# First attention of a two-layer model: k's halves swapped per key tile, projections moved behind score products

## The reference

```python
h = _layernorm(x, axis=-1) * (1 + ca) + sa
x = x + ga * _L0_attn_ref(h, ...)
...
x = _rmsnorm(tokens, norm_w)
q = (x @ Wq).reshape(b, n, QH, DH).transpose(0, 2, 1, 3)
kv = x @ Wkv
k = kv[..., :H * DH].reshape(b, n, H, DH).transpose(0, 2, 1, 3)
v = kv[..., H * DH:].reshape(b, n, H, DH).transpose(0, 2, 1, 3)
q = _mh_rmsnorm(q, q_gamma)
k = _mh_rmsnorm(k, k_gamma)
q = q.reshape(b, H, g, n, DH)
sim = jnp.einsum('bhgid,bhjd->bhgij', q, k)
sim = jnp.tanh(sim / SOFTCLAMP) * SOFTCLAMP
sim = sim * DH ** (-0.5)
sim = jnp.where(causal, neg, sim)
attn = jax.nn.softmax(sim, axis=-1)
out = jnp.einsum('bhgij,bhjd->bhid', attn, v)
out = out.transpose(0, 2, 1, 3).reshape(b, n, H * DH)
return out @ Wout
```

## Time and profile before

| | us |
|---|---|
| median of 3 runs | 1952.88 (1952.42 to 1953.05) |
| profiled execution | 1955.93, of it span 1954.2 |
| PE busy | 1891.4 (97%) |
| PE weight loads | 1323.5 (68%) |
| VectorE busy | 1588.3 (81%) |
| ScalarE busy | 1443.6 (74%) |
| GpSimd busy | 674.2 (35%) |

### The profile page before, as it was taken

The page is one execution under the profiler, slowest core; times in us unless marked ns, Lnnn a source line. Parts: engine busy times, 40 slices in busy tenths (PEclk is TensorE's granted clock), DMA queues, the critical chain, the costliest instruction groups (busy, mean ns, idle before and its releaser), DMA issues. The chain is left out here.

```text
span 1954.2 us, 41236 instructions
## 1 busy us (share of the span) xinstructions
PE 1891.4 (97%) x14878; PEld 1323.5 (68%) x14878; DVE 1588.3 (81%) x3865; ACT 1443.6 (74%) x2020; POOL 674.2 (35%) x956
## 2 busy tenths in 40 slices
PE   7999999999999999998899999899999978999998
PEld 4788888888888888887344444677777753444443
DVE  6888888888888888873776775699999977888886
ACT  3888888888888888884677777466767755666665
POOL 1555555555555555552000000255555540000000
PEclk7999999999999999998999999899999999999999
DMA  2501111011110111100675554100000000000000
GB/s 96 127 22 28 29 28 28 15 28 29 29 28 15 29 28 29 26 23 1 138 174 119 111 120 99 45 2 2 2 3 2 2 2 6 12 11 17 12 17 17
DMA packets 57001, 75.67 MB, mean 39 GB/s; under 512 B 9456, under 2 KB 34144, under 8 KB 56672
## 3 DMA queue, kind: packets, MB, share of 16 engines
q1 hardware_dynamic: 56800, 73.03, 15.7%
HBM read 51.47 MB, written 4.77 MB: 29 GB/s over the span
## 5 line engine op out<-in xcount | busy, mean ns | idle before, releaser
L513 PE MATMUL a_pS<-qs,k 128*128 128x256 f16 x1536 | 377.2, 273 | 3.7 <-issue 2.6
L533 PEld LDWEIGHTS a_pO<-va,pr 128*128 128x128 f32 x2048 | 322.9, 192 | 82.1 <-issue 72.9
L533 PE MATMUL a_pO<-va,pr 128*128 128x66 f32 x2048 | 332.3, 252 | 3.1 <-DVE on L857 2.5
L1083 POOL TENSOR_SCALAR_AFFINE_SELECT pr<-pr 128x512 f32<-128x512 f32 x256 | 181.7, 734 | 192.4 <-ACT pr L1009 192.3
L1001 ACT ACTIVATE th<-a_pS 128x1536 f32<-128x1536 f32 x128 | 185.8, 1451 | 68.1 <-PE a_pS L513 65.2
L1982 ACT ACTIVATE c_pr<-c_pS 128x2048 f32<-128x2048 f32 x96 | 180.4, 1879 | 59.8 <-PE c_pS L1785 59.8
L2026 POOL TENSOR_SCALAR_AFFINE_SELECT c_pr<-c_pr 128x512 f32<-128x512 f32 x256 | 155.5, 638 | 181.9 <-DVE c_pr L1875 181.9
L513 PEld LDWEIGHTS a_pS<-qs,k 128*128 128x128 f16 x1536 | 196.3, 131 | 7.3 <-issue 4.0
L864 POOL TENSOR_TENSOR qp<-qg,qp 128x1024 f16<-128x1024 f32 x64 | 149.2, 2331 | 121.5 <-ACT qp L977 121.5
L1009 ACT ACTIVATE pr<-th 128x1536 f32<-128x1536 f32 x128 | 189.6, 1481 | 1.1
L535 PEld LDWEIGHTS a_pO<-va,pr 128*128 128x128 f32 x1024 | 162.5, 192 | 31.4 <-issue 28.7
(11 more groups left out here) (267 smaller groups left out, 4336.2 us busy)
## 6 DMA issues: line engine op xcount, KB each, us to landing
b_cwB<-b_by_expert SPq DMA_DIRECT2D x64, 512.0 KB, 8.5
k<-k SPq DMA_DIRECT2D x64, 256.0 KB, 3.7
x<-in_L_attn_tokens_dram SPq DMA_DIRECT2D x8, 512.0 KB, 6.9
out_dram<-x SPq DMA_DIRECT2D x16, 256.0 KB, 2.3
mb<-a_by_sample SPq DMA_DIRECT2D x31, 128.0 KB, 3.5
d_h<-in_L_ffn_h_w_dram SPq DMA_DIRECT2D x2, 1024.0 KB, 8.2
c_gb<-c_by_sample SPq DMA_DIRECT2D x1, 2048.0 KB, 8.3
b_by_expert<-b_cwT SPq DMA_DIRECT2D x64, 8.0 KB, 1.4
```

The costliest lines, as they stand in the source:

```text
L513: last = pe.matmul(out, (k1, k2)[part][k][:, h // G2, keys * P:(keys + 1) * P], q, start=part == 0, stop=part == 1)
L533: last = pe.matmul(out, w[:, hh * N + t * P:hh * N + (t + 1) * P], v[:, 0, p, :], start=True, stop=t == 0)
L1083: last = gp.affine_select(out=own, in_=own, compare_op=ALU.is_ge, fill=0.0, base=0, pattern=[[0, HPG], [1, P]], channel_multiplier=-1)
```

## The change

Four things in `attention0`:

1. `k1` and `k2` are laid out by key tile first, and SP swaps k's halves in two transfers per key tile, each pair issued as soon as that tile's copy is done. Score product 0 of a sample waits for the copy of tile 0 alone, product 1 for its transfers, product 4 for the copy of tile 1 and product 5 for its transfers.
2. The loop of PE is written out in another order; so are those of VectorE, ScalarE and GpSimd, which begin at another point of the sample. The calls are the same and as many.
3. The banks are given out in another way, and with them the waits at the head of the calls.
4. `act_take_k` writes its tile of `k1` as one run of 1024 elements.

```diff
-        k1 = [sb(f'k1{k}', [P, KH, N], F16) for k in range(2)]
+        k1 = [sb(f'k1{k}', [P, TT, KH, P], F16) for k in range(2)]
...
-        QK_BANK = (1, 0, 1, 1, 0, 2)
+        QK_BANK = (1, 0, 1, 2, 1, 2)
...
-                sp.wait_ge(s_ks, 2 * n + 2)
-                sp.dma_start(k2[k][0:DH, :, :], k1[k][DH:P, :, :]).then_inc(s_k2, 16)
-                sp.dma_start(k2[k][DH:P, :, :], k1[k][0:DH, :, :]).then_inc(s_k2, 16)
+                for t in range(TT):
+                    sp.wait_ge(s_ks, 2 * n + t + 1)
+                    sp.dma_start(k2[k][0:DH, t, :, :], k1[k][DH:P, t, :, :]).then_inc(s_k2[t], 16)
+                    sp.dma_start(k2[k][DH:P, t, :, :], k1[k][0:DH, t, :, :]).then_inc(s_k2[t], 16)
...
             elif m == 3:
                 if n >= 1:
+                    pe.wait_ge(s_ks, 2 * n)
+            elif m == 4:
+                if n >= 1:
                     pe.wait_ge(s_qs, 4 * n - 3)
...
-                    pe.wait_ge(s_k2, 32 * (n + 1))
+                    pe.wait_ge(s_ks, 2 * n + 1)
...
+            if g == 0:
+                if m == 1:
+                    pe.wait_ge(s_k2[0], 32 * (n + 1))
+                elif m == 4:
+                    pe.wait_ge(s_ks, 2 * n + 2)
+                elif m == 5:
+                    pe.wait_ge(s_k2[1], 32 * (n + 1))
...
-                pe_weigh(pe, n, 1, 10)
-                pe_project_qk(pe, n + 2, 3)
-                pe_weigh(pe, n, 1, 11)
                 pe_project_qk(pe, n + 2, 4)
                 pe_project_qk(pe, n + 2, 5)
...
-            act.activation(k1[n % 2][:, :, t * P:(t + 1) * P], pW[KT_BANK[t]][:, :].bitcast(F16).rearrange('p (h i) -> p h i', i=P), ACT.Copy).then_inc(s_ks, 1)
+            act.activation(k1[n % 2][:, t, :, :], pW[KT_BANK[t]][:, :].bitcast(F16).rearrange('p (h i) -> p h i', i=P), ACT.Copy).then_inc(s_ks, 1)
```

More of the change, by code:

```diff
@@ L355, in attention0 @@
         s_qt, s_qs, s_kt, s_ks = (sem(x) for x in ('qt', 'qs', 'kt', 'ks'))
[L356 removed]
+        s_v, s_va = (sem(x) for x in ('v', 'va'))
+        s_k2 = [sem(f'k2{t}') for t in range(TT)]
         s_sc, s_th, s_pr, s_mk, s_pv, s_rl, s_on, s_as = (
@@ L404, in pe_values @@
             if t == 0:
+                if n >= 1:
+                    pe.wait_ge(s_qs, 4 * n - 1)
+                else:
+                    pe.wait_ge(s_hT, n + 2)
+            else:
                 if n + 1 < B:
@@ L417, in pe_project_qk @@
             if m == 0:
-                pe.wait_ge(s_hT, n + 1)
+                if n >= 1:
+                    pe.wait_ge(s_qg, 6 * n - 1)
             elif m == 1:
-                if n >= 2:
-                    pe.wait_ge(s_qs, 4 * n - 5)
+                if n >= 1:
+                    pe.wait_ge(s_va, 2 * n - 1)
+                else:
+                    pe.wait_ge(s_hT, n + 1)
+            elif m == 2:
+                if n >= 3:
+                    pe.wait_ge(s_at, 2 * n - 4)
                 elif n >= 1:
-                    pe.wait_ge(s_qg, 6 * n - 1)
-            elif m == 2:
-                if n >= 1:
                     pe.wait_ge(s_va, 2 * n)
@@ L455, in pe_turn_k @@
                 if n + 1 < B:
[L456 to L459, removed]
-                if n + 1 < B:
                     pe.wait_ge(s_qg, 6 * n + 8)
                 else:
-                    pe.wait_ge(s_qs, 4 * n - 1)
+                    pe.wait_ge(s_va, 2 * n + 1)
+            else:
+                if n >= 2:
+                    pe.wait_ge(s_og, n - 1)
+                elif n >= 1:
+                    pe.wait_ge(s_qs, 4 * n)
+                else:
+                    pe.wait_ge(s_qg, 6 * n + 6)
             out = pW[KT_BANK[t]][:, :].bitcast(F16)
@@ L474, in pe_turn_q @@
             if i == 0:
-                pe.wait_ge(s_ks, 2 * n + 1)
+                if n + 1 < B:
+                    pe.wait_ge(s_qg, 6 * n + 9)
+                else:
+                    pe.wait_ge(s_at, 2 * n - 2)
             elif i == 1:
-                pe.wait_ge(s_ks, 2 * n + 2)
+                if n >= 2:
+                    pe.wait_ge(s_st, 3 * n - 5)
+                else:
+                    pe.wait_ge(s_ks, 2 * n + 1)
             elif i == 2:
-                if n + 1 < B:
-                    pe.wait_ge(s_qg, 6 * n + 11)
+                if n + 2 < B:
+                    pe.wait_ge(s_hT, n + 3)
                 else:
@@ L512, in pe_score @@
                 out, q = pS[:, hh * N:(hh + 1) * N], qs[k][:, h, :]
-            last = pe.matmul(out, (k1, k2)[part][k][:, h // G2, keys * P:(keys + 1) * P], q, start=part == 0, stop=part == 1)
+            last = pe.matmul(out, (k1, k2)[part][k][:, keys, h // G2, :], q, start=part == 0, stop=part == 1)
             if m == SCORES - 1:
@@ L547, in pe_heads_back @@
                     else:
-                        pe.wait_ge(s_st, 3 * n - 2)
+                        pe.wait_ge(s_og, n)
                 else:
-                    pe.wait_ge(s_at, 2 * n + 1)
+                    if n + 2 < B:
+                        pe.wait_ge(s_va, 2 * n + 6)
+                    elif n + 1 < B:
+                        pe.wait_ge(s_qs, 4 * n + 5)
+                    else:
+                        pe.wait_ge(s_at, 2 * n)
             last = pe.transpose(pW[HB_BANK[t]][:, j * P:(j + 1) * P], as_[:, t, j * P:(j + 1) * P], c.id32[:, :])
@@ L579, in pe_out_back @@
                 pe.wait_ge(s_og, n + 1)
-                pe.wait_ge(s_og, n + 1)
+                if n + 2 < B:
+                    pe.wait_ge(s_ks, 2 * n + 5)
+                elif n + 1 < B:
+                    pe.wait_ge(s_qs, 4 * n + 7)
+                else:
+                    pe.wait_ge(s_st, 3 * n - 2)
             last = pe.transpose(pW[BACK_BANK][:, t * P:(t + 1) * P], og[:, t * P:(t + 1) * P], c.id32[:, :])
@@ L657, in _ @@
                 pe_turn_k(pe, n + 1, 0)
-                pe_score(pe, n, 3, 2)
-                pe_weigh(pe, n, 1, 6)
-                pe_score(pe, n, 3, 3)
+                for m in range(1, 6):
+                    pe_score(pe, n, 3, m)
+                    pe_weigh(pe, n, 1, m + 1)
                 if n == -1:
@@ L711, in _ @@
                 pe_weigh(pe, n, 3, 0)
[L712 to L719 removed]
+                pe_turn_q(pe, n + 1, 2)
+                pe_turn_q(pe, n + 1, 3)
+                for m in range(0, 11):
+                    pe_score(pe, n + 1, 1, m)
+                    pe_weigh(pe, n, 3, m + 1)
+                pe_score(pe, n + 1, 1, 11)
+                pe_values(pe, n + 2, 0)
+                pe_heads_back(pe, n, 0, 0)
+                pe_values(pe, n + 2, 1)
+                pe_weigh(pe, n + 1, 0, 0)
+                pe_score(pe, n + 1, 2, 0)
+                pe_weigh(pe, n + 1, 0, 1)
+                pe_score(pe, n + 1, 2, 1)
+                pe_weigh(pe, n + 1, 0, 2)
         def dve_ln(dve, n, step):
```

216 lines of the change are left out of this document (86 added, 130 removed).

## The result

The changed kernel takes 1922.44 us in the median (four runs, 1920.92 to 1925.79), the one before 1952.65 beside it. The ratio is 0.9848, 95% interval 0.9831 to 0.9865: faster by 30.2 us, where 25.8 were forecast. Run again later on one chip with the kernel before, it took 0.9844 (0.9829 to 0.9860) of it. The profiled execution took 1925.79 us (span 1924.0), the slowest of its four.

A forecast was written before the change was run, and what follows sets the result against it. TensorE's instruction stream was taken as the bound, 26.95 us a sample. Order 23.5 plus swap 3.8 less new waits 1.5 gave 25.8 us: 1930.1 profiled, 1927 in the median, range 1921 to 1942.

The forecast's parts named there:

- The cost of an f32 instruction behind a short one: TensorE's stream: f32 straight behind a weighing product or turn pays 0.053 us; reordering saves 0.78 a sample, 23.5 us.
- P after S: A projection straight after a score product on TensorE: taken as 0.86 us, between bounds of 0.86 and 0.91.
- the rival in which the projection still pays: Projections behind scores on TensorE still pay 0.053 each; 11 us not won, 1938 us; chance 0.16.
- full cover by loads pulled ahead: TensorE's weight loads always hidden, so order is free; only the swap's 3.8 us remain, 1949 us; chance 0.04.
- The swap: A sample's first score product waits for transfers of k's halves; splitting them wins 3.8 us, at worst none.
- the spare time: Between k's transfers landing and the score needing them: 1.3 us spare in the median, 0.5 at the slowest landing.
- New waits, -1.5: TensorE waiting for ScalarE's tanh between score groups: 0.05 us once a sample, 1.5 us lost; bounds 0 and 13.
- The spare time claimed: Blocks between score groups: tanh needs 1.81 us, blocks last 2.00, 2.04 and 2.11, so 0.2 to 0.3 spare.
- Filling and draining counted at nothing: First and last samples of the stage: TensorE also waits for other engines there, so no gain was counted.
- short pairs: f32 instructions straight after a weighing product or turn on TensorE: 15 a steady sample before, none after.
- VectorE as the bound: Rival: VectorE, 23.1 us of work a sample, has its waits add up and becomes the limit; 1960 us, chance 0.05.

The follow-up runs named there:

- The three kernels that bring it back: Changed kernel with five weighing products behind weighing products: 1928.97 us; three output products behind weighing products: 1926.34 us; two projections behind weighing products: 1926.36 us.
- the kernel that had the drain's clock at 1.00: Kernel before, with ten idle transpositions filling TensorE's 1.16 us wait in the last sample: 1950.94 us, ratio 0.9996 to the kernel before.

## Why the prediction was right, and where it was off

**The cost of an f32 instruction behind a short one: right, in rule and in size.** The three kernels that bring it back give 0.053 (W), 0.052 (O) and 0.053 (P). "P after S" was a value chosen between bounds of 0.86 and 0.91; it is 0.86, so the rival in which the projection still pays falls, and with it full cover by loads pulled ahead. The Trainium skill, "TensorE: Matmul & The Clock Gate", Step-by-step: what each phase is for, states that the next tile's weights load while this tile's matmul runs. With weighing products in pairs PE's stream lengthens by 0.26 us a sample and PE waits for nothing, so as full cover that doesn't hold for these short matmuls; the measurement decides. The term was 0.78 a sample, and 26.84 less 26.07 is 0.77.

**The swap: right in the size, too simple in the reason.** 3.8 us of waits are gone, 3.5 of them seen alone in the 28 intervals, and 0.95 in the last sample that the forecast hadn't counted. But I priced it as an amount in the kernel before. In the new order the same whole transfers would cost 14.6 us, since the first score of a sample comes 0.3 sooner after k's second copy. The forecast missed nothing by this, because the changed kernel has the split; with the order alone I'd have been 10 us wrong, as the expectation for that kernel was. The half-size transfer, priced like the whole (3.7), lands in 2.3, so by the forecast's own sum the spare time was 2.7 and not 1.3.

**New waits, -1.5: mis-sized, none came.** From 88 to 850 us the view lists not one idle interval of PE. The spare time claimed, 0.2 to 0.3 at three places, is 0.12 at one and 0.23 at two; the value of 0.05 a sample was caution, not a reading.

**Filling and draining counted at nothing: the main miss.** The step was "PE also waits for other engines, so I count nothing there". The forecast took 15 short pairs in each of 30 samples, 450. The stage has 505 before and 28 after, 477 fewer; 461 to 465 fewer show their 0.05, since waits cover some. That is 0.6 to 0.8 us more than forecast. The last sample's wait for the swap went as well. Both could have been counted as in the body. At equal clock the tail brought 2.0 us, net of new waits for the tanh; another 3.3 come from the clock, which was lower before in that one profile.

**The sum.** For the profiled executions: 25.2 in the body against a predicted 0.91 by 28, 25.5; plus 6.5 at both ends, less 1.6 in later stages, 30.1. For the medians: 30.2 against 25.8. The forecast had 25.5 for the body and 0.3 for the ends (two of its thirty samples, 1.8, less the 1.5 of new waits); measured are 25.2 and 5.0. Of the 5.0, the drain at equal clock is 2.0 and the head's short pairs 0.9; 2.1 stay open. The head's other waits and the clock at both ends may be in them, but the kernel that had the drain's clock at 1.00 wasn't faster in the median. No errors cancel in this: the cautious 1.5 and the ends both made the forecast low.

**VectorE as the bound** fell: its wait for q's turns shrank from 1.7 to 0.34 us a sample, and new waits for ScalarE's squares came (54.3 us), all while PE ran without a gap.

## What to carry to other kernels

Where TensorE has no idle time, look at start-to-start intervals by what stands ahead: an f32 product behind a 128x66 or 128x128 one paid 0.053 us here that it didn't pay behind a 256-column score. A reordering worth 0.77 us a sample cost nothing but the room of other chains, so recount how long each chain has after it: the wait that was worth 0.13 a sample was worth 0.5 in the new order. Count the stages' ends too, with the same rule as the steady part.

## What the runs showed that I had not expected

- Halving a transfer within SBUF from 256 to 128 KB cut its landing from 3.7 to 2.3 us in the median, and moved the slowest from 4.4 to 5.2, by kernel, to 3.6 to 4.2. The Trainium skill, "DMA: Bandwidth & Descriptors", Anatomy of one DMA — SWDGE (gpsimd) path, has a fixed cost of about 2.0 us plus bytes by 436e3, an estimate of 2.6 and 2.3 for these two. These transfers are issued by SP and not on that path; the half agrees, the whole takes 1.1 more.
- PE's interval was the same to 0.01 us in all 28 samples, so a change of 0.1 us at one place of a sample could be read from one profile, where the median of a few runs barely tells 3 us.
- The granted clock fell in a draining stretch of the kernel before, behind waits of 0.95 to 1.30 us. In another profile the first two of these waits stand and the clock stayed at 1.00. Its cause stays open.
